# A reordered software pipeline: the loop order of five engines, the output sum cut in two, and the extremes in seven pieces

## The reference

```python
shift = silu(causal_depthwise_conv(x, conv_w, 4 taps) + conv_b)
r, k  = split(shift @ in_proj_w.T)                    # 64 and 64 columns
u     = sigmoid(x @ w0.T @ w1.T + b1) * x             # rank 128
sel, tau = softplus(...), sigmoid(...)                # from shift @ mem_gate_w.T
g, k  = -sel * tau, k / norm(k) * sel ** tau
S_t   = exp(g_t) * S_(t-1) + k_t u_t                  # state 64 x 1024, along the sequence
o_t   = r_t S_t / 8
y     = layernorm(x + o + shift * res_w)              # then a second block:
xf    = layernorm(y) * gamma + beta
tile  = the best of 64 slices of 16 channels, by the signs of xf (8 clusters of 8)
mn, mx = least and greatest xf of each tile's slice, over ALL rows that chose the tile
delta = spline(tile, (x_slice - mn) / (mx - mn)) * output_scale[tile]
out   = layernorm(y + y + delta in the 16 chosen channels)
```

## Time and profile before

| what | us |
|---|---|
| median of 3 runs | 1265.76 (1264.2 to 1268.58) |
| the profiled execution | 1264.53 |
| its span, first to last instruction | 1262.8 |
| PE busy | 1111.0 (88%) |
| DVE busy | 1084.7 (86%) |
| ACT busy | 943.7 (75%) |
| POOL busy | 818.6 (65%) |

### The profile page before, as it was taken

How to read it: one execution, slowest core, us unless ns; L and a number is a source line. 1 busy time by engine, 2 the same in 40 slices (tenths; PEclk the granted TensorE clock), 3 DMA queues, 4 the chain that set the end, 5 groups by cost and what they waited for, 6 DMA issues and landing times. The chain is left out here.

```text
span 1262.8 us, 31497 instructions
## 1 busy us (share of the span) xinstructions
PE 1111.0 (88%) x9278; PEld 714.4 (57%) x9278; DVE 1084.7 (86%) x2538; ACT 943.7 (75%) x1805; POOL 818.6 (65%) x1647
## 2 busy tenths in 40 slices
PE   5799999999999999999999999999999997835510
PEld 4456666666666666666666666666666663421000
DVE  4898888898989898989999898999899977788874
ACT  4757888888888888888888888888888875415863
POOL 3125666676767676767676767676767666534675
PEclk8999999999999999999999999999999998666555
DMA  4112222222222222222222222222222213958999
GB/s 146 34 39 105 107 107 107 107 105 105 105 105 105 105 105 105 105 105 105 104 104 104 96 95 96 103 104 105 105 105 95 95 68 107 396 197 339 407 419 385
DMA packets 63650, 174.88 MB, mean 138 GB/s; under 512 B 11435, under 2 KB 22643, under 8 KB 63606
## 3 DMA queue, kind: packets, MB, share of 16 engines
q1 hardware_dynamic: 52118, 149.33, 31.8%
q10 hardware_dynamic: 5984, 23.07, 4.5%
q0 software_dynamic: 5504, 1.94, 1.0%
HBM read 69.06 MB, written 101.04 MB: 135 GB/s over the span
## 5 line engine op out<-in xcount | busy, mean ns | idle before, releaser
L1190 DVE SCALAR_TENSOR_TENSOR acc<-xT_all,cw_sb,acc 128x256 f32<-128x256 f32 x768 | 354.0, 519 | 6.8 <-ACT acc L849 6.8
L876 ACT ACTIVATE sg<-TS,bet,gam 128x256 f16<-128x256 f32 x244 | 123.3, 556 | 26.7 <-PE TS L493 26.7
L513 PE MATMUL PR<-xT_all,w_sb 128*128 128x256 f32 x512 | 137.3, 392 | 3.4 <-ACT xT_all L812 3.4
L525 PE MATMUL WKB<-w_sb,tS 128*128 128x512 f32 x256 | 137.4, 618 | 0.0
L849 ACT ACTIVATE acc<-xT_all,cb_sb,cw_sb 128x256 f32<-128x256 f32 x256 | 132.5, 591 | 4.9 <-DVE xT_all L1176 2.9
L595 PE MATMUL PR<-shT,w_mg_sb 128*64 128x128 f32 x2048 | 128.8, 280 | 6.6 <-ACT shT L858 6.6
L368 POOL TENSOR_TENSOR AT<-AT,Wm 128x128 f32<-128x128 f32 x210 | 108.0, 514 | 39.5 <-DVE AT L1216 24.8
L567 PE MATMUL OB<-th_all,AT 128*128 128x512 f32 x256 | 123.4, 605 | 5.8 <-DVE AT L368 2.0
L595 PE MATMUL PR<-shT,w_rk_sb 128*64 128x128 f32 x2048 | 125.9, 276 | 0.0
L595 PEld LDWEIGHTS PR<-shT,w_rk_sb 128*64 128x64 f32 x2048 | 110.5, 137 | 25.7 <-issue 25.7
L595 PEld LDWEIGHTS PR<-shT,w_mg_sb 128*64 128x64 f32 x2048 | 113.4, 139 | 19.0 <-issue 12.0
(11 more groups left out here) (274 smaller groups left out, 2744.4 us busy)
## 6 DMA issues: line engine op xcount, KB each, us to landing
xin_all<-in_x SPq DMA_DIRECT2D x32, 1024.0 KB
y_ring<-y_all SPq DMA_DIRECT2D x32, 1024.0 KB, 4.1
y_scratch<-y_all SPq DMA_DIRECT2D x32, 1024.0 KB, 6.1
own<-y_scratch SPq DMA_DIRECT2D x5, 2048.0 KB, 17.1
rows<-y_scratch SPq DMA_DIRECT2D x4, 2048.0 KB, 13.3
out<-rows ACTq DMA_DIRECT2D x8, 1024.0 KB, 18.5
out<-own ACTq DMA_DIRECT2D x6, 1024.0 KB, 18.9
RX<-RE SPq DMA_DIRECT2D x128, 32.2 KB
```

The lines of the kernel that those rows point to most:

```text
L513: i = pe.matmul(PR[:, 0:T], w0_sb[:, blk, :], xT[b][:, blk, HIST:HIST + T], start=(blk == 0), stop=(blk == NB - 1))
L525: pe.matmul(WK[h][:], tS[b][:, chunk_cols(c)], w1_sb[:, half_cols(h)], start=True, stop=False)
L876: nc.scalar.activation(sg[:, blk, :], at[:, (blk % 2) * T:(blk % 2 + 1) * T], ACT.Sign, scale=gam[:, blk:blk + 1], bias=bet[:, blk:blk + 1 ...
L1190: v.scalar_tensor_tensor(acc[:, blk, :], xT[b][:, blk, i:i + T], cw_sb[:, blk, i:i + 1], acc[:, blk, :], ALU.mult, ALU.add).then_inc(e_con ...
```

## The change

Three things change. First, the order of the calls in the five `step` functions and with it the stages at which the steps are cut; the drain is fitted to it. Second, `output` is cut into `out_products` (L567 and L572) and `out_reads` (L570); for chunk 0 the products come first, for chunk 1 the reads. Third, the extremes have seven pieces with other bounds. The operations on the data are the same, and as many.

```diff
-    EXT_ENDS = (4, 24, 33, 48, 60, 64)
+    EXT_ENDS = (4, 8, 34, 44, 52, 60, 64)
...
-                def output(c, k, b):
+                def out_products(c, k, b):
                     done(pe, e_res[1], k)
+                    done(pe, e_AT, k)
+                    wait(pe, e_u[c], k)
+                    for h in range(2):
+                        pe.matmul(OB[:, half_cols(h)], AT[:, c, :], th[b][c][:, half_cols(h)], start=(c == 0), stop=False)
+                    for blk in range(NB):
+                        i = pe.matmul(OB[:, blk * P:(blk + 1) * P], zT[b][:, blk, chunk_cols(c)], ident[:],
+                                      is_transpose=True, start=False, stop=(c == 1 and blk % 4 == 3))
+                    if c == 1:
+                        i.then_inc(e_o[c].sem, 1)
+
+                def out_reads(c, k, b):
                     pe.wait_ge(d_rx, (k + 1) * 64)
                     if c == 0:
                         earlier(pe, e_S[1], k, 1)
                     else:
                         wait(pe, e_S[0], k)
...
                     for h in range(2):
                         rows = chunk_rows(h)
-                        pe.matmul(OB[:, half_cols(h)], RX[rows, c, 0:CH], S[c][rows, :], start=False, stop=False)
...
+                        i = pe.matmul(OB[:, half_cols(h)], RX[rows, c, 0:CH], S[c][rows, :], start=(c == 1), stop=(c == 0))
+                    i.then_inc(e_o[c].sem if c == 0 else e_r1.sem, 1)
...
                 def decay(c, k, b):
...
                     if c == 0:
-                        earlier(dve, e_o[1], k, 1)
+                        earlier(dve, e_r1, k, 1)
                         earlier(dve, e_S[1], k, 1)
                     else:
                         wait(dve, e_o[0], k)
...
-                pipeline(act, step, NG + 1, 4)
+                pipeline(act, step, NG + 1, 3)
...
-                chunk_decay(*own(LAST - 1))
-                norm_max(*own(LAST))
                 masked(0, *own(LAST - 1))
                 masked(1, *own(LAST - 1))
+                assemble(dve, v, *own(LAST - 1))
+                norm_max(*own(LAST))
                 gates_ratio(*own(LAST))
-                assemble(dve, v, *own(LAST - 1))
...
                 log_scale(*own(LAST))
+                gate(1, *own(LAST))
                 key_norm(*own(LAST))
...
+                extremes(4, 8)
                 decay(0, *own(LAST))
                 for c in range(CPG):
                     normed(c, *own(LAST - 1))
-                extremes(4, 24)
+                extremes(8, 34)
                 best_key(*own(LAST - 1))
                 choice(*own(LAST - 1))
                 for c in range(CPG):
                     normed(c, *own(LAST))
-                extremes(24, 33)
+                extremes(34, 44)
                 best_key(*own(LAST))
                 choice(*own(LAST))
-                extremes(33, 48)
-                extremes(48, 60)
+                extremes(44, 52)
+                extremes(52, 60)
                 extremes(60, NC)
...
-                pipeline(pool, step, NG - 2, 2, NG // 2 - 1)
+                pipeline(pool, step, NG - 1, 3, NG // 2 - 1)
```

More of the change, by code:

```diff
@@ L749, in _ @@
                 reads_done((e_y[1], LAST - 2))
-                output(0, *own(LAST - 1))
+                out_products(0, *own(LAST - 1))
+                out_reads(0, *own(LAST - 1))
                 reads_done((e_xev[3], LAST), (e_km, LAST - 3), (e_at0[1], LAST - 1))
@@ L754, in _ @@
                 reads_done((e_y[0], LAST - 1))
-                output(1, *own(LAST - 1))
+                out_reads(1, *own(LAST - 1))
+                out_products(1, *own(LAST - 1))
                 reads_done((e_sg[0], LAST - 2))
@@ L767, in _ @@
                 reads_done((e_y[1], LAST - 1))
-                output(0, *own(LAST))
+                out_products(0, *own(LAST))
+                out_reads(0, *own(LAST))
                 reads_done((e_km, LAST - 2), (e_at0[1], LAST))
@@ L772, in _ @@
                 reads_done((e_y[0], LAST))
-                output(1, *own(LAST))
+                out_reads(1, *own(LAST))
+                out_products(1, *own(LAST))
                 reads_done((e_S[0], LAST))
@@ L1404, in step @@
                     if live(g, 2):
[L1405 removed]
+                        log_scale(*of(2))
                     if live(g, 1):
[L1407 to L1433 removed]
+                        conv_round(0, 2, *of(1))
+                        conv_round(0, 3, *of(1))
                     if live(g, 4):
@@ L1437, in step @@
                     if live(g, 1):
-                        gate(1, *of(1))
+                        conv_round(1, 1, *of(1))
+                        conv_round(1, 2, *of(1))
+                    if live(g, 2):
+                        key_norm(*of(2))
+                    if live(g, 1):
+                        conv_round(1, 3, *of(1))
+                    if live(g, 2):
+                        read_key(*of(2))
+                        keys_scaled(*of(2))
+                        chunk_decay(*of(2))
+                        reads_scaled(*of(2))
+                    if live(g, 1):
+                        residual(0, *of(1))
+                        gate(0, *of(1))
+                        residual(1, *of(1))
+                    if live(g, 2) and not last:
+                        masked(0, *of(2))
+                    if live(g, 1) and not last:
+                        norm_max(*of(1))
+                    if live(g, 2) and not last:
+                        masked(1, *of(2))
+                    if live(g, 3) and not last:
+                        normed(0, *of(3))
+                    if live(g, 1) and not last:
+                        gates_ratio(*of(1))
                     if first(g - 2):
```

299 lines of the change are left out of this document (133 added, 166 removed).

## The result

The changed kernel takes 1231.92 us (median of 4 runs, 1231.72 to 1233.01) where the kernel before takes 1264.98 beside it: a ratio of 0.973, 95% interval 0.971 to 0.975. The forecast was 1231, in a range of 1221 to 1248. Its profiled execution took 1231.75 us, 32.8 less than the one before; the forecast difference was 34.9.

A forecast was written before the change was run, and what follows sets the result against it. PE, busy without a gap, was taken to bound the loop. Savings of 9 + 19.6 + 1.6 + 0.3 + 4.4 = 34.9 us took profiled execution from 1264.5 to 1229.6, so a median of 1231, range 1221 to 1248.

The forecast's parts named there:

- first groups: Start of the loop: groups 0 and 1 reach their first reads sooner, saving 9 us (bounds 0 and 12).
- 28 periods: Loop on PE: each period 0.70 us shorter, 32.38 to 31.68, saving 19.6 us (bounds 0 and 26).
- last step: Loop's last step: two fills are missing and ACT had waited before; saves 1.6 us (bounds 0 to 2.5).
- drain to the last choice: Drain: earlier products, mostly taken back by extremes(8, 34) ahead of best_key; saves 0.3 us (bounds -2 to +2).
- behind the last choice: End of drain: extremes pieces of 8, 8, 4 columns instead of 15, 12, 4; saves 4.4 us (3.5 to 4.5).
- second block: After the drain: unchanged, its 143 us move as a whole, so no gain or loss.
- Narrow runs: PE in the loop: 64-column or 64-row matmul runs cost 0.16 to 0.31 us each; three fewer save 0.70 a period.
- Rival 2: POOL's gathers stall beside two-input VectorE operations and POOL becomes the bound: period 33.5, 1281 us, slower; chance 0.07.
- Rival 1: Loop: a wait enters PE and the period falls back toward 32.38; 1241 with half the gain, 1250 with none; chance 0.22.
- Rivals 3 and 4: 3: first groups gain 12, period reaches 31.5, 1223 us, chance 0.06. 4: order does nothing, 1261 us, chance 0.03.

The follow-up runs named there:

- old_ends: Changed kernel with only the pieces of the extremes put back to those of the kernel before: 1241.82 us.
- split: Changed kernel with gate_product(3) put between the two projection passes, one narrow run more per group: 1242.87 us.
- best: late_breaks with joined's PE order and tables_idle's spline tables: 1221.12 us, ratio 0.966 to the kernel before.
- tables_idle: Changed kernel with slope_signs and the spline tables (5.7 us) moved into VectorE's idle time: 1231.55 us.
- late_breaks: late with ten one-column copies a group strewn into VectorE's row of two-input operations: 1232.46 us.
- late: Changed kernel with key_norm ahead of best_key, and VectorE's key and read products behind the first residual and gate: 1372.22 us.
- late_split: split with late's move of VectorE's products: 1372.34 us.
- late_tables: tables_idle with late's move of VectorE's products: 1370.92 us.
- joined: Changed kernel with states(1) and out_reads(0) directly behind states(0), two narrow runs fewer per group: 1235.71 us.
- late_pairs: late_breaks with its ten one-column copies a group made into one-column products of two tensors: 1283.17 us.
- breaks_split: late_breaks with gate_product(3) put between the two weights of the first projection pass, as in split: 1256.75 us.

## Why the prediction was right, and where it was lucky

In the order of its sum, each term as the two traces have it:

| term | forecast | measured | from |
|---|---|---|---|
| first groups | 9 | 7.2 | t_blocks of group 31 27.0 earlier, less the loop |
| 28 periods | 19.6 | 19.8 | 907.3 to 887.5 us, keys to keys |
| last step | 1.6 | 1.1 | squares_sum(31) 28.1 earlier |
| drain to the last choice | 0.3 | 0.4 | choice(31) 28.5 earlier |
| behind the last choice | 4.4 | 4.35 | 15.5 us for 19.8; 19.9 in old_ends |
| second block | 0 | 0 | 142.8 and 142.7 us |

The sum was 34.9 us; the profiled executions differ by 32.8. The medians agree better, 1231 and 1231.92, by luck: the forecast took over the 1.2 us by which the profiled execution of before lies under its median, and that of the changed kernel lies 0.2 under.

**Narrow runs.** Right, in kind and in size: three fewer gave 0.70 us; one more gave 0.30 (split), two fewer 0.43 (best, in the blocks; 0.23 in the period). From each line's start to the next one's on PE, the 0.70 lies in the projections (7.59 us a period before, 7.29 after), the transposes of x (0.15 less), those of z (0.11), the products with AT (0.10) and of the norms (0.10), all of them narrow runs or blocks beside one; the rest changes by 0.04 or less. With the kernels on both sides of the changed one this is shown and not only fitting. By the Trainium skill, "TensorEngine Tiling (Array Packing)", "Key Properties", a change of the tiling mode drains the array. The page gives no price, and no trace here shows a drain as such; what the runs show is 0.2 to 0.3 us for a narrow run, in and out.

**The first groups** are the term that was mis-sized. By t_blocks of group 4 it is 7.5 us (131.34 for 138.83). The reads of groups 0 and 1 came at 32.1 and 61.6, 8.1 and 7.3 earlier; 33.6 and 59.9 were forecast. The load behind gate(1) was named, and PE waited 5.76 us for it. That the spline tables hold up group 2 was named too, but counted as equal in both: tau_exp waits 5.97 for them at 74.25, and group 2 to 3 takes 36.0 us, where t_blocks had 33.1 before. tables_idle got that back, 5.7 us.

**Rival 2** holds the terms that failed without showing in the time. The mechanism was put rightly: POOL stands still beside an operation of VectorE with two tensors of SBUF. Three of its terms were off. The gathers took 6.2 us for the forecast 5. The slack behind them was smaller: even with gathers of 5.1 us, in late_breaks, squares(1) waits 0.30 us for mean(1), which was to be 0.6 early, and ACT has 0.91 at gates_in, not 1.4. And gates_in may come late, which wasn't counted: 1.0 us behind the projection's end cost nothing in old_ends, 1.2 cost 0.35. The last two nearly cancel. By the rival the period grows once the gathers take 2.0 us more than 5; it grew between 2.5 more (nothing) and 2.6 more (0.35 us in every second group of tables_idle). And in late, where the gathers take 3.8 to 5.4 us more than in the changed kernel, the period is 37.2 in its longest run and 36.55 and 36.73 in late_split and late_tables, past the 34.9 that was worked out for the hardest case: PE's lower clock comes on top. By the Trainium skill, "SBUF — State Buffer", "SBUF: two separate sides", a VectorE operation with two SBUF inputs contends with a POOL operation that reads SBUF, and the one that starts first holds the shared pair for its whole instruction. Here a gather was held through 13 instructions in a row, and ended while another such product ran (537.50 to 538.72 in late). By the Trainium skill, "SBUF — State Buffer", "Who interferes with whom", such products leave the generation of descriptors alone ("needs the write interface: inferred"). The 7.18 us don't decide on that, since these gathers also read their row numbers from SBUF, and the trace doesn't show which part of them stood.

**Rival 1** (a wait falls into the gap) came true in old_ends, split, joined and tables_idle, through ACT behind the gathers and not by slower signals. That the changed kernel escaped it in all groups but one was not in the argument: luck. Rivals 3 and 4 fell with the terms above.

**What stays open.** Why a gather passes in one group and not in another that starts it at the same place, and which property of the short operations lets it through. And what halts PE in late_pairs and breaks_split: those pauses, and four in old_ends and one in joined, all begin between 0.4 us ahead of the fourth gather's start and 1.2 behind it, and only where the gathers are short; changed, split, late_breaks and best have none, though their short gathers lie beside the same passes. Between 280 and 980 us no transfer of instructions is recorded in the traces of the changed kernel, breaks_split and late_pairs. Neither was tried further.

## What to carry to other kernels

Where PE is the bound and has no gap, count how often its shape changes: each separate run of 64-row or 64-column matmuls cost 0.2 to 0.3 us beyond its own work, and putting two together gave it back, unless a wait took it (half of it in best). Before a gain in a full loop is believed, look for the chain with no slack left (here gather, mean, squares, table, gates): an edit elsewhere may tip it, as old_ends did for 5 us in a loop that it doesn't touch, and is then judged for that, not for what it does. Gathers from POOL don't belong beside an unbroken row of two-input VectorE operations; if they must stand there, a one-column operation ahead of every second one opened it here, for 0.07 us each; look for pauses of PE afterwards, which two of the four kernels with it had.

## What the hardware showed that was not expected

- A gather of 0.94 to 1.3 us took 7.18 us beside a row of 19 two-input operations, and 0.94 to 1.26 beside the same operations with a short one ahead of every second (late_breaks, from group 1 on).
- Four gathers took 6.2 or 7.5 us in otherwise equal groups that started them at the same place of VectorE's row, to a nanosecond.
- PE paused 0.3 to 1.8 us in nearly every group inside a run of matmuls without waits, in two kernels whose PE code differs in nothing (late_pairs) or one swap (breaks_split) from one that has no such pause.
